# Turning only the down weight by transposing DMA, and starting the first rows of the ternary FFN earlier

## What is computed

```python
def _weight_quant(w):
    scale = 1.0 / jnp.clip(jnp.mean(jnp.abs(w)), 1e-05)
    return jnp.clip(jnp.round(w * scale), -1.0, 1.0) / scale
def _act_quant(x):
    scale = 127.0 / jnp.clip(jnp.max(jnp.abs(x), axis=-1, keepdims=True), 1e-05)
    return jnp.clip(jnp.round(x * scale), -128.0, 127.0) / scale
def _bitlinear(x, w):
    return jnp.einsum('bsi,oi->bso', _act_quant(x), _weight_quant(w))
gate = silu(_bitlinear(x, w_gate)); up = _bitlinear(x, w_up)      # 512 -> 2048
x = x + _bitlinear(gate * up, w_down)                             # 2048 -> 512, x is layer-normed going in
```

## Time and profile before

| | us |
|---|---|
| median of 3 runs | 2025.44 (2023.45 to 2026.13) |
| the profiled execution, whole | 2025.38 |
| its span | 2023.7 |

### The profile page before, as it was taken

One profiled execution on the slowest core, in us unless ns is written; L12 is line 12 of the kernel. 1 busy time (PEld: TensorE's weight loads), 2 busy tenths in 40 slices (PEclk: granted clock), 3 DMA queues, 4 the chain that ended last, 5 costly groups with the idle time before them and its releaser, 6 DMA issues.

```text
span 2023.7 us, 43948 instructions
## 1 busy us (share of the span) xinstructions
PE 1938.5 (96%) x14011; PEld 1483.8 (73%) x14044; DVE 1324.0 (65%) x4073; ACT 1046.0 (52%) x2717; POOL 786.4 (39%) x1437
## 2 busy tenths in 40 slices
PE   5999999999999789999999999999999999999998
PEld 4788888888888544444447888888888877788876
DVE  4777777777776677788865565565656566454475
ACT  3677767776777644554444544544445443222252
POOL 2445545454546735455542122122221213222264
PEclk8999999999999899999999999999999999999999
DMA  5132113111314436665552112111121137222131
GB/s 195 41 122 77 60 67 112 60 60 71 109 57 168 141 92 179 173 151 137 137 115 91 43 51 77 42 62 64 42 83 43 42 120 235 74 94 83 63 125 43
DMA packets 184075, 192.28 MB, mean 95 GB/s; under 512 B 96240, under 2 KB 106480, under 8 KB 183936
## 3 DMA queue, kind: packets, MB, share of 16 engines
q1 hardware_dynamic: 183936, 190.66, 30.2%
HBM read 136.08 MB, written 33.57 MB: 84 GB/s over the span
## 4 chain that ended last, share of the span: by engine, by line
PE 86%; DVE 7%; issue 2%; ACT 2%; DMA 1%; POOL 1%; DVEq 0%; SPq 0%; ACTq 0%; POOLq 0%
PE bank L1028 19%; PE bank L1017 18%; PE bank L2503 12%; PE bank L1700 11%; PE bank L1083 7%; PE bank L1713 5%; PE bank L1096 5%; PE bank L1066 4%; PE bank L1008 2%; DVE c_probs L800 1%; PE bank L2409 1%; DVE c_pT L809 1%; DVE c_cT L764 1%; ACT c_probs L617 1%; DVE c_xnT L764 0%
## 5 line engine op out<-in xcount | busy, mean ns | idle before, releaser
L496 POOL TENSOR_SCALAR a_probs<-a_probs,a_rinv 128x256 f32<-128x256 f32 x512 | 238.6, 486 | 282.6 <-DVE a_rinv L816 282.6
L617 ACT ACTIVATE a_probs<-a_probs,a_negm 128x256 f32<-128x256 f32 x512 | 254.6, 502 | 116.8 <-DVE a_negm L800 116.1
L496 POOL TENSOR_SCALAR c_probs<-c_probs,c_rinv 128x256 f32<-128x256 f32 x128 | 67.5, 538 | 400.4 <-DVE c_rinv L816 400.3
L800 DVE CUSTOM_DVE_ANT_0 a_probs<-bank,a_mbias 128x256 f32<-128x256 f32 x512 | 191.6, 417 | 6.5 <-PE bank L1066 4.5
L2503 PE MATMUL bank<-m_xnT,m_s 128*128 128x512 f32 x768 | 184.7, 391 | 2.7 <-DVE m_hid L2244 2.7
L809 DVE COPY a_pT<-bank 128x512 f32<-128x512 f32 x128 | 88.2, 689 | 141.6 <-PE bank L1083 141.4
L617 ACT ACTIVATE c_probs<-c_probs,c_negm 128x256 f32<-128x256 f32 x256 | 127.4, 502 | 88.8 <-DVE c_negm L800 88.8
L1083 PE MATMUL bank<-a_ident,a_probs 128*128 128x128 f32 x1024 | 155.8, 275 | 14.1 <-POOL a_probs L496 7.1
L2503 PEld LDWEIGHTS bank<-m_xnT,m_s 128*128 128x128 f32 x768 | 142.6, 188 | 33.5 <-DVE m_hid L2244 3.1
L1083 PEld LDWEIGHTS bank<-a_ident,a_probs 128*128 128x128 f32 x1024 | 122.4, 142 | 31.7 <-issue 10.5
L1700 PE MATMUL bank<-b_wg,b_xqT 128*128 128x512 bf16 x501 | 131.0, 382 | 6.3 <-DMA b_xqT<-b_xq 5.6
(11 more groups left out here) (279 smaller groups left out, 4449.3 us busy)
## 6 DMA issues: line engine op xcount, KB each, us to landing
m_ew<-in_L_ffn_w_dram SPq DMA_DIRECT2D x24, 512.0 KB, 8.4
a_cbuf<-in_ctx_dram SPq DMA_DIRECT2D x16, 512.0 KB, 6.4
a_xbuf<-in_x_dram SPq DMA_DIRECT2D x16, 512.0 KB, 5.8
a_resb<-in_x_dram SPq DMA_DIRECT2D x16, 512.0 KB, 3.7
x<-a_resb SPq DMA_DIRECT2D x16, 512.0 KB, 2.8
b_xbuf<-x SPq DMA_DIRECT2D x32, 256.0 KB, 2.9
b_resb<-x SPq DMA_DIRECT2D x32, 256.0 KB, 3.1
x<-b_resb SPq DMA_DIRECT2D x32, 256.0 KB, 2.0
```

The source lines that it names most:

```text
L496: last = nc.gpsimd.tensor_scalar(pr, pr, rinv[:, s, r:r + 1], 0.0, ALU.mult, ALU.add)
L617: nc.scalar.activation(pr, pr, ACT.Exp, bias=negm[:, s, h % 2, t:t + 1], scale=-1.0, accum_out=ssum[:, s, QT * (h % 2) + t:QT * (h % 2) + ...
L800: nc.vector.tensor_tensor_reduce(out=probs[:, s, h % 2, t], in0=s_bank[h][:, t * SEQ:(t + 1) * SEQ], in1=mbias[:, el.par], scale=-sm_scale ...
```

## The change

The down weight isn't turned by TensorE and VectorE any more. ScalarE writes its slices with the function Sign, which leaves -1, 0 or 1, in an order in which SP can turn them with eight transposing DMAs (turn_down, two for each slice) into wd. The eight turns on TensorE and VectorE in tiles 0 and 1 go. Gate and up banks are now 2, 4 and 3, 5 instead of 2, 6 and 3, 7, and TensorE's first gate product no longer waits for the last rows of the attention to be summed, only for its scores to be read.

The first rows go sooner. x tiles 0 and 1 are read in the last batch but one. Their statistics are in quad -4, their normalising in quad -2 and -1, and the scale and quantising of tile 0 in quad -1. Rounding of down slices 0 to 3 on GpSimd moves back: slice 0 from ahead of the last quad's end to behind that quantise, slices 1 to 3 behind the quantise of tile 1. ScalarE takes three down slices ahead of the first silus instead of two. On SP, turn_x of tile 0 stands ahead of the store of the attention's last rows. SP no longer waits there for the store to complete: that wait is in tile 24 of phase b. The slice gate 0 gets a place of its own in memory.

```diff
         store(Element(0, batches - 1, batches))
-        for par in range(2):
+        for par in range(2) if QUADS == 2 else ():
             sp.wait_ge(stored[par], batches // 2 * 16)
...
-            for n, places in enumerate(((96, 0, 4, 8), (12, 32, 36, 40), (188, 100, 104, 108)))]
+            for n, places in enumerate(((203, 0, 4, 8), (12, 32, 36, 40)))]
+    tern2 = [sb(f"tern2_{c}", at * KB, [P, KC, KC, P], BF16) for c, at in enumerate((188, 100, 104, 108))]
...
-    g_bank, u_bank = [banks[2], banks[6]], [banks[3], banks[7]]
+    g_bank, u_bank = [banks[2], banks[4]], [banks[3], banks[5]]
...
+    def turn_down(sp, c):
+        sp.wait_ge(w_integer, 2 * SLICES + c + 1)
+        for a in range(0, KC, 2):
+            sp.dma_start_transpose(wd[:, KC * c + a:KC * c + a + 2].rearrange("p a (o n) -> p (a o) n", n=P),
+                                   tern2[c][:, a:a + 2].rearrange("p a o n -> p (a o n)")) \
+              .then_inc(down_turned[c // 2], 16)
...
     def sync_beside(sp):
         sp.wait_ge(*prior.gone["context"])
         load_slice(sp, 0, 1)
+        sp.wait_ge(*prior.gone["xn"])
+        sp.wait_ge(prior.made["rows"][0], 16)
+        for el in first[:2]:
+            load_x(sp, el)
...
-        sp.wait_ge(w_turned, HALF)
-        sp.wait_ge(prior.made["rows"][0], 16)
-        for el in first[:2]:
-            load_x(sp, el)
         sp.wait_ge(*prior.gone["probs"])
         load_slice(sp, 2, 2)
         load_slice(sp, 2, 3)
+        sp.wait_ge(w_integer, 2 * SLICES)
+        turn_x(sp, first[0])
+        sp.wait_ge(prior.made["rows"][1], 16)
+        load_x(sp, first[2])
...
-        sp.wait_ge(prior.made["rows"][1], 16)
-        for el in first[2:]:
-            load_x(sp, el)
-        turn_x(first[0])
-        turn_x(first[1])
+        turn_x(sp, first[1])
+        load_x(sp, first[3])
+        sp.wait_ge(*prior.gone["all"])
+        turn_down(sp, 0)
+        turn_down(sp, 1)
         sp.wait_ge(w_turned, 4 * HALF)
         load_res(first[0])
+        turn_down(sp, 2)
+        turn_down(sp, 3)
...
-        elif step == -2:
+        elif step in (-3, -2):
+            normalise(pool, first[step + 3])
+        elif step == -1:
+            quantise_x(pool, first[0])
             rounded(pool, 2, 0)
-        elif step == -1:
-            normalise(pool, first[0])
-            normalise(pool, first[1])
-            rounded(pool, 2, 1)
...
-        quantise_x(first[0])
-        rounded(pool, 2, 2)
-        quantise_x(first[1])
-        rounded(pool, 2, 3)
+        quantise_x(pool, first[1])
+        for c in range(1, SLICES):
+            rounded(pool, 2, c)
         normalise(pool, first[2])
         round_h(first[0])
...
+        src = raw[n][c][:].rearrange("p (o a j) -> p o a j", o=KC, a=KC)
+        nc.scalar.activation(tern2[c].rearrange("p a o j -> p o a j"), src, ACT.Sign, bias=-MAGIC).then_inc(w_integer, 1)
...
-        integer(act, 2, 0)
-        integer(act, 2, 1)
+        for c in range(3):
+            integer(act, 2, c)
...
         silus(first[0], range(NC))
-        integer(act, 2, 2)
         integer(act, 2, 3)
...
     def vector_beside(dve, quad):
-        if quad == -3:
+        if quad == -4:
+            row_stats(dve, first[0])
+            row_stats(dve, first[1])
+        elif quad == -3:
...
             turned(dve, [5, 6, 7])
-            row_stats(dve, first[0])
-            row_stats(dve, first[1])
+            x_scale(dve, first[0])
     def vector_behind(dve):
         turned(dve, [10, 11])
-        x_scale(dve, first[0])
...
-        turned(dve, [12, 13])
         x_scale(dve, first[1])
-        turned(dve, [14, 15])
+        turned(dve, [12, 13, 14, 15])
...
             for half in range(HALVES):
+                if el.n == 0:
+                    pe.wait_ge(down_turned[half], 4 * 16)
...
-        pe.wait_ge(*prior.gone["all"])
+        pe.wait_ge(*prior.gone["scores"])
         pe.wait_ge(w_out, 4 * HALF)
         gate_up(first[0], range(NC))
...
-                gate_up(el.plus(1), [0, 1])
-                turn(pe, range(4 * HALF, 5 * HALF))
-                gate_up(el.plus(1), [2])
-                turn(pe, range(5 * HALF, 6 * HALF))
```

More of the change, by code:

```diff
@@ L1226, in ternary_ffn_phase @@
          "consts_ready ident_zero").split()]
+    down_turned = [sem(f"down_turned{half}") for half in range(2)]
     w_loaded = [[sem(f"w_loaded{i}_{c}") for c in range(SLICES)] for i in range(3)]
@@ L1276, in load_slice, with turn_x @@
         sp.dma_start(raw[n][c][:].rearrange("p (t c) -> p t c", c=DIM), cut).then_inc(w_loaded[n][c], 16)
+    def turn_down(sp, c):
[4 more added lines that the diff above has]
+              .then_inc(down_turned[c // 2], 16)
+    def turn_x(sp, el):
+        wait_apart(sp, u_done, (el.n - 1) * NC)
+        wait_apart(sp, xq_ready, el.n + 1)
+        sp.dma_start_transpose(xqT[:, el.par], xq[:, el.par]).then_inc(tx_out[el.par], 16)
     def pieces_of(el):
@@ L1362, in iteration @@
                 beside.sync_beside(sp, el.n)
+            if el.n == tiles - 8:
+                for stores in prior.made["rows"]:
+                    sp.wait_ge(stores, BATCH // 2 * 16)
             if el.has(4):
@@ L1460, in iteration @@
             if el.has(2):
-                quantise_x(el.plus(2))
+                quantise_x(pool, el.plus(2))
             if el.has(3):
@@ L1474, in integer @@
         wait_for(act, w_integer, PLACE_FREE[n * SLICES + c])
-        nc.scalar.activation(tern[n][c][:], raw[n][c][:], ACT.Copy, bias=-MAGIC).then_inc(w_integer, 1)
+        if n < 2:
+            nc.scalar.activation(tern[n][c][:], raw[n][c][:], ACT.Copy, bias=-MAGIC).then_inc(w_integer, 1)
+            return
+        src = raw[n][c][:].rearrange("p (o a j) -> p o a j", o=KC, a=KC)
+        nc.scalar.activation(tern2[c].rearrange("p a o j -> p o a j"), src, ACT.Sign, bias=-MAGIC).then_inc(w_integer, 1)
     def scalar_beside(act, quad):
         if quad == -6:
-            act.wait_ge(*prior.gone["xn"])
             integer(act, 0, 0)
@@ L1617, in hidden @@
                     largest(c - 1)
-                if isinstance(el.n, int) and el.n == 1 and c in (1, 2):
-                    turned(dve, range((3 + c) * HALF, (4 + c) * HALF))
             largest(NC - 1)
@@ L1707, in down @@
                 beside.tensor_beside(pe, el.n)
-            if isinstance(el.n, int) and el.n == 0:
-                pe.wait_ge(w_out, len(turns))
+            if el.n == 0:
+                pe.wait_ge(*prior.gone["all"])
             for half in range(HALVES):
+                if el.n == 0:
+                    pe.wait_ge(down_turned[half], 4 * 16)
                 pe.wait_ge(th_out[half][el.par], el.dma())
@@ L1720, in iteration @@
         def iteration(el):
-            if isinstance(el.n, int) and el.n == 0:
-                gate_up(el.plus(1), [0, 1])
-                turn(pe, range(4 * HALF, 5 * HALF))
-                gate_up(el.plus(1), [2])
-                turn(pe, range(5 * HALF, 6 * HALF))
-            elif el.has(1):
-                gate_up(el.plus(1), range(NC - 1))
-            if beside and number(el) == tiles - 1:
+            if el.has(1):
+                gate_up(el.plus(1), range(NC))
+            if beside and el.n == tiles - 1:
                 beside.tensor_units(pe)
-            if el.has(1):
-                gate_up(el.plus(1), range(NC - 1, NC))
             down(el, beside)
```

27 lines of the change are left out of this document (10 added, 17 removed).

## The result

The changed kernel takes 2014.0 us (median of 5 runs, 2012.33 to 2015.5), the kernel before beside it 2024.7 us (5 runs, 2023.45 to 2026.13). The ratio is 0.9947, with a 95% interval of 0.9933 to 0.9962: 10.7 us less. Forecast was 12.7 less. The profiled execution took 2015.28 us with a span of 2013.6 us; the one of before 2025.38 and 2023.7. The difference of the two spans is 10.1 us. The sign, the waits and the order of the chain came out as forecast; one term of the sum was too small, and the experiments are mostly about that term.

What follows compares the result with a forecast made beforehand. TensorE, busy 96% of the 2023.7 us span, was taken as the bound. Tile 0 ending 13.5 us sooner (+0.3 included), less 0.8 for the clock, gave 2025.4 - 12.7 = 2012.7 us; range 2009.2 to 2018.3, own range 2010.5 to 2015.

Steps and rivals of the forecast that it cites:

- The tail of the attention: End of the first attention: probabilities scaled late on GpSimd cost +0.3 us (0 to 1.3); last output product ends at 692.4.
- The start of tile 0: First gate product of the ternary FFN starts at 697.0 instead of 701.86, so 4.9 us sooner.
- start brings nothing: Rival: SP or GpSimd keeps the first gate product near 701.86, only the turning goes; 11.1 us less, 2014.3; chance 0.13.
- What that start is worth: Tile 0's gate and up: first silu at 703.0, last product multiplied from 707.35 instead of 710.02, 2.7 us sooner.
- The rest of tile 0: Tile 0's down product ends at 720.0 instead of 733.55, 13.5 us; TensorE's clock takes back 0.8 (0 to 2.5).
- (1) SP: SP's queue: eight transposing DMAs at 1.23 us each, 9.9 us; SP free 0.8 us before the hidden rows' transpose.
- (2) The DMA engines: Down weight's eight transposes take at most 1.8 us each, 14 us, fitting in the 20 us between 697.6 and 718.
- rival of serial transposes: Transposing DMAs served one after another: no change at 3.4 us each, 17 us slower (2042) at 5.1; chance 0.08.
- (3) Sign slices: ScalarE's down slices with Sign take 1.9 us each, upper bound twice that.
- rival of dear slices: A Sign slice on ScalarE takes 3.8 us, first silu at 706.8, some 5 us lost, 2018; chance 0.10.
- (4) The last slice: ScalarE's last down slice, 707.1 to 709.0 between silus of tiles 0 and 1, is covered by 2.3 us before the integers.
- The rule on tables: If Sign needed another table set, 1.28 us more ahead of tile 1's first silu would make the time 2014.0.

Runs made afterwards that it cites:

- Experiment 4: Changed kernel with GpSimd's roundings of down slices 1 and 2 moved ahead of the quantise of row tile 1: 2012.38 us, ratio 0.9936 to the kernel before.
- The execution with a length of 28.1 us: Changed kernel repeated with no edit, 2016.26 us; length runs from the end of attention's last output product to the end of tile 0's down product.
- experiment 2: Changed kernel with 14 and 10 unread dummy products filling TensorE's waits in tiles 0 and 1: 2013.95 us, ratio 0.9955 to the kernel before.
- experiment 6: Its last kernel: the changed kernel with GpSimd's roundings ahead of row tile 1's quantise and ten filling products in tile 1's wait: 2012.26 us, ratio 0.9941.
- experiment 1: Kernel before with only the down weight turned by Sign and eight transposing DMAs, first rows at the old places: 2018.08 us, ratio 0.9968.
- experiment 3: Changed kernel with ScalarE doing down slice 2 behind tile 0's silus instead of ahead: 2014.43 us, ratio 0.9956 to the kernel before.

## Why the prediction was right, and where it was off

**The tail of the attention (+0.3).** The first turning of probabilities starts at 678.64 instead of 678.44, and the last output product ends at 692.36; forecast was 692.4. Right.

**The start of tile 0 (697.0).** Measured 697.18. The transpose of the first rows is issued at 687.80, and what came last was VectorE's emptying of turned up weight (1.88 us of wait at 695.15), as argued. The rival "start brings nothing" is out. One reading behind it was too simple: the prediction says that the attention's last rows stood at 693.00 on VectorE because GpSimd's addition of the bias ended at 692.93. VectorE itself was busy until 692.98, and it is this row that the chain of before goes through:

```profile
691.67 1.31 DVE b_xs L1575
```

The two ended within 0.05 us of each other, so the sum isn't touched by it; the last section comes back to the row.

**What that start is worth.** The chain came out step for step: roundings to 699.8 (699.7), slice to 701.77 (701.7), table load 1.28, first silu at 703.06 (703.0), wait of TensorE to 703.81 (703.8). Only the 16 products behind it took 5.33 us and not 3.5. The last hidden piece is therefore at 709.16, not 707.35; of the 2.7 us that the start was to give there, 0.9 were left. Experiment 4 confirms by an edit that it was GpSimd's queue, not ScalarE's slices, that held the silu.

**The rest of tile 0, where the step failed.** The term was "I take 0.8 (0 to 2.5)" for TensorE's clock. It measured 3.7 us in the profiled execution, beyond its bound of 2.5. The mechanism was named and the size was wrong. The prediction itself had worked out that eight slow products behind the first wait cost 1.7 us; they cost 1.88. It then took half of that, and it charged nothing for the second wait, which it had at 2.3 us and which cost 1.84 more. I had only the rows behind 5.62 us of waiting, and took a wait of less than half that for harmless. The trace of before has one more place that was not read, behind the stop of 5.45 us:

```profile
723.14 1.90 PE L1700 MATMUL bank<-b_wu,b_xqT 128*128 128x512 bf16 x4
```

It gives the price of a slow group, 1.90 us; but no full-size product of that trace was slow behind a short wait, so that a wait of 2.25 us can be followed by one had to be measured. With 3.7 in place of 0.8 the end of tile 0 is at 723.7; it is at 723.58. Nothing else is missing from the sum. By it the profiled execution would be 2025.4 - 9.8 = 2015.6 us, and it took 2015.28. That is just outside the forecast's own range; the median of 2014.0 lies inside it, which is in part luck. The execution with a length of 28.1 us has the term at 0.5 (27.6 without any), so 0 to 3.7 would have been its range. Since such executions lost 1.5 to 3.9 us behind tile 0, the time doesn't follow them. Whether the two belong together is open. The two executions with a length of 28.1 us are also the two with the slowest product behind L967 (6.03 and 6.07). Other runs speak against a link: the filled kernel of experiment 2 and the first of experiment 4 had both third pieces warm too, and 5.31 and 5.09 us for that product, and the last one of experiment 6 was warm at both places (26.9 us of length, 3.63 for that product).

**The added work.** (1) SP: 1.34 us for an issue right behind another, instead of 1.23. The slack of 0.8 us behind the slices is there (713.42 to 714.20), both ends 1.8 us later than forecast, but a read of x stands in it, which I had left out, so 0.16 remains; two issues more cost 1.4 us. (2) The DMA engines: landings 3.3 us for the down weight's and the hidden rows' alike. The rival of serial transposes, which would have given a loss, is out. (3) Sign slices: 1.90 us, 3.86 for two; the rival of dear slices is out. (4) The last slice, 708.88 to 710.8, is covered by the 2.36 us ahead of the integers. (5) The eight emptyings and 64 transposes are gone with their 6.7 us of waits; alone that is worth 6.9 us, less than the 11.1 of the first rival (the times allow 4.3 to 8.9). That rival left out that slices issued late hold the hidden rows on SP (experiment 1), so early start and turning by DMA are not two separate gains.

**The rule on tables.** There is one table load in this passage, at 701.77, behind three Sign slices, and none around the fourth, which stands between two groups of silus. By the list in "Table sets: the hidden batching unit" of the page "ScalarE: Activation LUTs" in the Trainium skill, which doesn't name Sign, a second load was to be feared. Here it didn't come. The load's row of 1.28 us agrees with what the section "What ACT_TABLE_LOAD costs" of that page gives for the load itself; the drain by which that section comes to 2.66 us isn't seen, for there is no gap before the load or behind it.

**The chances.** The likeliest case held; its own range (2010.5 to 2015) has the 2014.0. But the time alone fits the rival "start brings nothing" (2014.3) as well, and a second table load (2014.0) exactly; only the trace parts them, with a start at 697.18 and one load.

## What to carry to other kernels

Cost a new wait of TensorE twice: the wait, and slow products behind it, at the rate of a slow row of the same kernel (1.9 against 1.03 us here), for each wait, also for short ones; then say that an execution may or may not pay it. When work moves from a compute engine to DMA, count its issues on the queue that sends them and look who stands behind: here eight issues of 1.34 us, and the hidden rows' transpose. And look at what an in-order engine has queued ahead of the thing that the critical engine will wait for: two roundings moved on GpSimd took away the largest wait that the change had left. Last, where one execution can differ from the next by 3 us in a passage, take several traces of one kernel before a difference of 1 or 2 us between two kernels is put down to an edit.

## What the runs showed of the hardware

The clock of one and the same instruction stream falls at different places from execution to execution. Of four profiled executions of the changed kernel, three had 1.2 GHz behind waits of 3.0 and 2.25 us, and one had the same 2.25 us wait with no fall behind it. The length of the wait alone doesn't decide: products were slow behind waits of 1.92 and 1.97 us (experiment 1, and the slice moved back in experiment 3), and at full speed behind one of 1.78 us (experiment 6) and behind 2.25 us in all executions whose slow groups stood at the start. Another low stretch came behind 32 products of one column (3.6 to 4.4 us) and a wait of 0.27 or 0.67 us: the down product there took 4.8 to 6.0 us in the four executions of the changed kernel, and 3.63 in the last one of experiment 6.

A small VectorE instruction got ten times dearer beside one of GpSimd. In the kernel before, two TENSOR_TENSOR of one column on VectorE took 2.37 us while GpSimd added the bias with TENSOR_TENSOR; in the changed kernel, where they no longer coincide, 0.21 us. The kernel that only turns by DMA kept the old place, and there the pair took 2.35 us beside GpSimd's 2.53. First before, then after:

```profile
690.61 2.37 DVE L1575 TENSOR_TENSOR b_xs<-b_xmax,b_wscale 128x1 f32<-128x1 f32 x2
```

```profile
694.19 0.21 DVE L1591 TENSOR_TENSOR b_xs<-b_xmax,b_wscale 128x1 f32<-128x1 f32 x2
```

That GpSimd's instruction is the cause was not tried by itself: the place of the pair moved together with much else. In the kernel before the second of the two stands in the chain that ended last (the row of 691.67 above), ahead of the attention's last rows; in the changed kernel it isn't in that chain.
